# Loading replicated rows with one transfer per piece over all partitions instead of one per block of partitions

## The reference

```
e  = stack(tbl_f[ids[:, f]] for f in 0..38)              # (512, 39, 16)
z0 = relu(einsum('bhd,bkd,hks->bsd', e, e,  w0) + b0)     # 128 maps; first 64 are x1, the rest is summed
z1 = relu(einsum('bhd,bkd,hks->bsd', e, x1, w1) + b1)     # x2 and a summed half
z2 = relu(einsum('bhd,bkd,hks->bsd', e, x2, w2) + b2)     # all 128 summed
z  = sum over d of (z0[64:], z1[64:], z2)                 # 256 numbers per sample
y  = relu(relu([z, dense_ctx] @ W1 + c1) @ W2 + c2) @ W3
```

## Time and profile before

| | |
|---|---|
| median of the runs | 657.21 us |
| the profiled execution | 660.38 us, its span 658.6 us |
| granted TensorE clock over the span | 0.987 of full speed |
| TensorE matmuls busy | 613.0 us, 93% of the span |
| VectorE, ScalarE, GpSimd busy | 83%, 62%, 81% |
| moved by DMA | 78.60 MB, a mean of 119 GB/s |
| SyncE's DMA queue | 75.11 MB, 54.9% of the time of 16 DMA engines |

### The profile page before, as it was taken

How to read it: one execution, slowest core, us unless ns; L and a number is a source line. 1 busy time by engine, 2 the same in 40 slices (tenths; PEclk the granted TensorE clock), 3 DMA queues, 4 the chain that set the end, 5 groups by cost and what they waited for, 6 DMA issues and landing times.

```text
span 658.6 us, 6385 instructions
## 1 busy us (share of the span) xinstructions
PE 613.0 (93%) x1996; PEld 378.3 (57%) x1996; DVE 546.7 (83%) x616; ACT 410.6 (62%) x553; POOL 536.2 (81%) x325
## 2 busy tenths in 40 slices
PE   0169899999999999999999999999999999999998
PEld 0026465666656566656666666666566666655563
DVE  1248699898989898998989898989989898969740
ACT  2025857676676758576766757586777667575622
POOL 6657899898989899998989998999989886747520
PEclk9998899999999999999999999999999999999899
DMA  6689794938374756749384747567494847420000
GB/s 220 136 191 187 160 172 98 180 73 184 89 147 109 139 104 132 148 101 179 71 165 107 146 100 140 114 126 154 95 180 75 162 110 134 96 46 1 0 0 0
DMA packets 53216, 78.60 MB, mean 119 GB/s; under 512 B 39081, under 2 KB 42025, under 8 KB 49891
## 3 DMA queue, kind: packets, MB, share of 16 engines
q1 hardware_dynamic: 47566, 75.11, 54.9%
q0 software_dynamic: 5120, 1.29, 2.0%
q10 hardware_dynamic: 496, 1.80, 1.1%
HBM read 76.23 MB, written 1.94 MB: 119 GB/s over the span
## 4 chain that ended last, share of the span: by engine, by line
PE 38%; POOL 38%; ACT 11%; issue 6%; DMA 4%; DVE 3%; SPq 1%; DVEq 0%; ACTq 0%
POOL low L361 29%; PE z L681 20%; PE z L698 9%; POOL gat L351 9%; ACT x L448 7%; PE z L713 6%; ACT high L428 2%; DMA spread<-x_rows 2%; DVE prod L591 2%; DMA gat<-table_dram,index 2%; ACT r L472 1%; DMA x_rows<-gat 1%; DVE base L626 1%; DVE low L634 1%; PE base L758 1%
## 5 line engine op out<-in xcount | busy, mean ns | idle before, releaser
L361 POOL TENSOR_TENSOR low<-prod,high 128x1024 fp32r<-128x1024 f32 (+2 forms) x160 | 380.7, 2399 | 58.8 <-ACT high L428 57.7
L591 DVE TENSOR_TENSOR prod<-spread,x 128x1024 f32<-128x1024 f32 (+1 forms) x256 | 307.6, 1212 | 38.7 <-ACT x L448 37.7
L681 PE MATMUL z<-prod,w_sb 128*128 128x512 f32 (+3 forms) x608 | 294.0, 604 | 36.9 <-DVE prod L572 32.4
L428 ACT ACTIVATE high<-prod 128x1024 fp32r<-128x1024 f32 (+2 forms) x160 | 167.7, 1058 | 116.9 <-DVE prod L591 98.4
L698 PE MATMUL z<-high,high_w_L 128*128 128x512 f32 (+1 forms) x448 | 205.9, 459 | 1.0 <-ACT high L438 1.0
L713 PE MATMUL z<-low,high_w_L 128*128 128x512 f32 (+1 forms) x448 | 182.6, 488 | 5.5 <-POOL low L361 3.5
L681 PEld LDWEIGHTS z<-prod,w_sb 128*128 128x128 f32 (+3 forms) x608 | 116.2, 192 | 124.0 <-issue 101.6
L351 POOL DMA_INDIRECT gat<-table_dram,index x160 | 154.7, 967 | 37.0 <-issue 35.3
L698 PE MATMUL z<-high,low_w_L 128*128 128x512 f32 (+1 forms) x448 | 179.0, 400 | 0.0
L448 ACT ACTIVATE x<-z,bias_sb 64x512 f32<-64x512 f32 (+1 forms) x186 | 120.2, 646 | 15.1 <-PE z L681 7.4
L713 PEld LDWEIGHTS z<-low,high_w_L 128*128 128x128 f32 (+1 forms) x448 | 82.8, 190 | 71.7 <-issue 45.8
(11 more groups left out here) (37 smaller groups left out, 62.4 us busy)
## 6 DMA issues: line engine op xcount, KB each, us to landing
spread<-x_rows SPq DMA_DIRECT2D x139, 192.0 KB, 13.5
spread<-x_rows SPq DMA_DIRECT2D x30, 546.0 KB
spread<-x_rows SPq DMA_DIRECT2D x47, 256.0 KB, 4.2
spread<-x_rows SPq DMA_DIRECT2D x15, 468.0 KB
x0base<-x_rows SPq DMA_DIRECT2D x47, 78.0 KB
gat<-table_dram,index POOLq DMA_INDIRECT x160, 5.6
x_rows<-gat SPq DMA_DIRECT2D x16, 72.0 KB, 2.2
wt_sb<-wt_dram SPq DMA_DIRECT2D x2, 512.0 KB, 19.0
```

Of the source, the lines that this page charges most:

```text
L361: pool.tensor_tensor(low[0:rows, h, 0:k, :], prod[0:rows, slot(c, kind, g), 0:k, :], high[0:rows, h, 0:k, :].bitcast(F32), ALU.subtract).t ...
L428: act.activation(high[0:rows, split_slot(c, kind, g), 0:k, :], prod[0:rows, slot(c, kind, g), 0:k, :], ACT.Copy).then_inc(high_ready, 1)
L591: dve.tensor_tensor(prod[0:rows, slot(c, kind, g), :, :], spread[0:rows, c % 2, g, :].unsqueeze(1).to_broadcast([rows, k, N]), x[0:rows, : ...
L681: last = pe.matmul(z[:, :], w[0:rows, at + j, :], prod[0:rows, slot(c, kind, g), j, :], start=g == 0 and j == 0, stop=closes and j == k - 1)
```

## The change

Every load of replicated rows becomes one transfer over all its partitions: one for `x0base` and one for `spread0` (117 partitions each), and one for each piece of `spread` (128 partitions), so 5 per chunk in place of 18. Their source patterns get a dimension in front: the three or four blocks. All of them are issued by SyncE, those of chunk 0 too; ScalarE's two helpers go. Semaphore counts follow (16 per transfer). The last blocks are loaded at full length (7 rows for 6, 10 for 9). `ROWS` is written another way and is 59 as before, so `store_x0` is unchanged.

```
-            def load_base(c, js=range(DPT)):
+            def load_base(c):
 ...
                 row = x0_dram[c, 0:1, 0:1]
-                for j in js:
-                    sp.dma_start(x0base[j * F:(j + 1) * F, :], bass.AP(row.tensor, row.offset, [[N, F], [1, N]])
-                                 ).then_inc(base_in, 16)
+                sp.dma_start(x0base[:, :], bass.AP(row.tensor, row.offset, [[0, DPT], [N, F], [1, N]])
+                             ).then_inc(base_in, 16)
 ...
-            def load_spread0(c, at, end, done, js=range(DPT)):
+            def load_spread0(c, at, end, done):
 ...
-                for j in js:
-                    many = min(end, DELTAS - j * T0) - at
-                    row = x0_dram[c, j * T0 + at:j * T0 + at + 1, 0:1]
-                    src = bass.AP(row.tensor, row.offset, [[N, F], [1, many * N]])
-                    sp.dma_start(spread0[j * F:(j + 1) * F, at:at + many, :].rearrange("p t n -> p (t n)"), src
-                                 ).then_inc(done, 16)
+                row = x0_dram[c, at:at + 1, 0:1]
+                src = bass.AP(row.tensor, row.offset, [[T0 * N, DPT], [N, F], [1, (end - at) * N]])
+                sp.dma_start(spread0[0:R0, at:end, :].rearrange("p t n -> p (t n)"), src).then_inc(done, 16)
 ...
-                for q in qs:
-                    many = min(end, F - q * G1) - at
-                    row = x0_dram[c, q * G1 + at:q * G1 + at + 1, 0:1]
-                    src = bass.AP(row.tensor, row.offset, [[0, QUAD], [1, many * N]])
-                    sp.dma_start(spread[q * QUAD:(q + 1) * QUAD, c % 2, at:at + many, :].rearrange("p g n -> p (g n)"),
-                                 src).then_inc(spread_in[p][c % 2], 16)
+                row = x0_dram[c, at:at + 1, 0:1]
+                src = bass.AP(row.tensor, row.offset, [[G1 * N, FPT], [0, QUAD], [1, (end - at) * N]])
+                sp.dma_start(spread[:, c % 2, at:end, :].rearrange("p g n -> p (g n)"), src
+                             ).then_inc(spread_in[p][c % 2], 16)
 ...
-            load_first()
             take_base(0)
-            load_first_spread()
```

More of the change, by code:

```diff
@@ L31 @@
 R0_LAST = (DPT - (DPT * T0 - DELTAS)) * F
-ROWS = F + FPT * (-(-(DELTAS - 1) // FPT))
+ROWS = F + FPT * (-(-max(DPT * T0 - 1, FPT * -(-F // FPT) - F) // FPT))
 G0 = -(-T0 // 2)
@@ L270, in load_base, with load_spread @@
                 row = x0_dram[c, 0:1, 0:1]
-                for j in js:
-                    sp.dma_start(x0base[j * F:(j + 1) * F, :], bass.AP(row.tensor, row.offset, [[N, F], [1, N]])
-                                 ).then_inc(base_in, 16)
-            def load_spread0(c, at, end, done, js=range(DPT)):
+                sp.dma_start(x0base[:, :], bass.AP(row.tensor, row.offset, [[0, DPT], [N, F], [1, N]])
+                             ).then_inc(base_in, 16)
+            def load_spread0(c, at, end, done):
                 if c >= 1:
                     sp.wait_ge(prod_done, PROD_NUMBER[c - 1, "L0", G0 - 1])
-                for j in js:
-                    many = min(end, DELTAS - j * T0) - at
-                    row = x0_dram[c, j * T0 + at:j * T0 + at + 1, 0:1]
-                    src = bass.AP(row.tensor, row.offset, [[N, F], [1, many * N]])
-                    sp.dma_start(spread0[j * F:(j + 1) * F, at:at + many, :].rearrange("p t n -> p (t n)"), src
-                                 ).then_inc(done, 16)
-            def load_spread(c, p, qs=range(FPT)):
+                row = x0_dram[c, at:at + 1, 0:1]
+                src = bass.AP(row.tensor, row.offset, [[T0 * N, DPT], [N, F], [1, (end - at) * N]])
+                sp.dma_start(spread0[0:R0, at:end, :].rearrange("p t n -> p (t n)"), src).then_inc(done, 16)
+            def load_spread(c, p):
                 at, end = PIECES[p]
@@ L312, in _ @@
             store_x0(0)
-            load_base(0, (0, 1))
+            load_base(0)
             for n, (at, end) in enumerate(FIRST_CUTS):
-                load_spread0(0, at, end, spread0_first[n], (0, 1))
+                load_spread0(0, at, end, spread0_first[n])
             for p in range(len(PIECES)):
-                load_spread(0, p, (0, 1))
+                load_spread(0, p)
             store_x0(1)
@@ L387, in split_weights @@
                                ).then_inc(high_w_ready, 1)
[L389 to L411, removed]
             def take_base(c):
-                act.wait_ge(base_in, 16 * DPT * (c + 1))
+                act.wait_ge(base_in, 16 * (c + 1))
                 if c >= 1:
@@ L565, in product0 @@
                     if c >= 1:
-                        dve.wait_ge(spread0_in, 16 * DPT * c)
+                        dve.wait_ge(spread0_in, 16 * c)
                 for n, (at, _) in enumerate(FIRST_CUTS):
                     if c == 0 and 2 * g == at:
-                        dve.wait_ge(spread0_first[n], 16 * DPT)
+                        dve.wait_ge(spread0_first[n], 16)
                 free_slot(c, "L0", g)
@@ L582, in wait_factors @@
                     if g == at and kind == "L1":
-                        dve.wait_ge(spread_in[p][c % 2], 16 * FPT * (c // 2 + 1))
+                        dve.wait_ge(spread_in[p][c % 2], 16 * (c // 2 + 1))
             def product(c, kind, g):
```

## The result

The changed kernel takes 1001.47 us (median of 4 runs, 999.87 to 1006.96), the kernel before 658.0 us in the same comparison. The ratio is 1.523, 95% interval 1.516 to 1.531: half as slow again. The forecast was 1310 us in a range of 980 to 1650. The direction and the small number of engines were right. The size was not: 1310 us is 31% too high, and the measured time lies near the lower edge of a wide range, close to rival B (990 us), which had a chance of 0.17.

A forecast was written before the change was run, and what follows sets the result against it. TensorE was taken to bound the kernel before, loads on three or four engines the changed one. Sixteen chunks at 73.0 us, fifteen gaps of 4, 24 at the start and 60 at the end gave 1312, stated as 1310 us, range 980 to 1650.

The forecast's parts named there:

- rival B: Loads of `spread`: confined to few engines, but these run free at 24.8 GB/s; 990 us in all, chance 0.17.
- The bound before: Steady state of the kernel before: TensorE busy 36.9 of 37 us sets the stage, DMA has 37% to spare.
- Three or four engines: All merged loads: the source's first count limits the cut, so 3 engines carry `x0base` and `spread0`, 4 carry `spread`.
- `x0base` and `spread0`, 25.7 us: Layer 0's loads per chunk on three engines at 24.8 GB/s each: 3.2 us for `x0base`, 22.5 us for `spread0`.
- `spread`, 46.5 us: Pieces of `spread` per chunk, 655 KB on the busiest engine at 14.1 GB/s; 26.4 us at 24.8 GB/s.
- The gap of 4 us: Between chunks: `x0base` waits for the store behind the last piece, so the three engines idle 4 us per stage.
- The ends: Start and tail of the span: first data at 24 us, and 60 us after the last piece has landed.
- Rival A: All merged loads: the cut follows the partitions alone, 16 or 13 engines, start 5 to 6 us sooner; 652 us, chance 0.13.

## Why the prediction was right, and where its size was off

**The bound before, right.** Runs that shorten the loads move nothing, runs that lengthen them past a stage move everything.

**Three or four engines, right, and now shown.** This was inferred from 39 rows on 13 engines. Three marks per `x0base`, 0.52 of the engines with a count of 8, and stages that grow with counts of 4 and 2 show it, at a fixed destination in the cases of 8 and 4. The Trainium skill (DMA: Bandwidth & Descriptors, "Why a DMA increments its semaphore by 16 and not by 1") has exactly this rule, and every run agrees. Its advice in "Rules for kernel authors" to use one transfer over 128 partitions and not two over disjoint halves does not carry over to this case by itself: merging was harmless with 39 in front and cost 147 us with 3.

**`x0base` and `spread0`, 25.7 us, right.** From the issue at 370.24 to the product at 397.83 pass 27.6 us, 28.3 in the mean of 15 stages, start and landing among them.

**`spread`, 46.5 us: the term that was mis-sized.** From layer 0's first product, when `spread0` is there, to the first use of the last piece pass 27.8 us in the mean of 15 stages (32.3 once, otherwise 25.2 to 29.8), near the 26.4 of rival B. I took the 14.1 GB/s of the 32-partition pieces for four engines because two of them walk partitions 0 to 63 side by side. The rate belonged to 13 to 16 engines that share one block of 32 partitions; eight on the same partitions have 25.1. My argument against B, that a sixth of the engines rested and the others were no faster, was wrong: 13 engines still shared one limit, about 190 GB/s together. The Trainium skill (SBUF — State Buffer, "Door 1: The DMA port swizzle") puts 32 partitions on 8 ports with 218 GB/s in all; 209 with eight engines and 190 with more agree. It also has partitions 0 to 31 and 32 to 63 on the same ports, and the long slow stretches (15.8, 17 and 17 GB/s, some 4 to 8 us) appear where engines work 32 apart; where four share a block, only some 2 us at the start are slow. I had assumed that such engines stay slow; they reach 25 GB/s within the same piece. That they are slow while they walk in step and slip out of it fits all this, but no run shows it, and the slow stretch in the middle of a piece shows that the pace can drop again.

**The gap of 4 us, right.** The next `x0base` is issued 1.4 us after the last piece is first used, in the mean, and its data move over 1 us later. The DMA share is 0.02 from 427 to 430 us. With 28.3 and 27.8 us these 1.4 us make 57.5 of the stage's 57.7. So some 3 us are empty, less than the 4.5 us that the run with the early store was expected to win.

**The ends, right.** The last piece is first used at 940.9 us of 1000.1: 59 us to the end for the 60 taken. The span is 20.7 us to the first issue, 15 x 57.7, and 113.9 from the last issue to the end, of which 54.7 are the last chunk's loads.

**Rival A** fell with the changed kernel's three marks and stages of 57.7 us. Its gain at the start did not come either: with 13 engines over the whole width the third product of chunk 0 begins at 35.7 us, not at 31. That load ran on 13 engines; 16 engines over 128 partitions for `spread` would need a source that begins with a larger count than its four blocks, and was not tried.

## What to carry to other kernels

Before merging transfers, write down the first count of both patterns: a replicating or blocked source with 3 or 4 in front left 12 or 13 engines idle here, and exchanging two dimensions (with the matching weight order) can bring them back. Then compare bytes per stage with engines x 25 GB/s. A low DMA share next to idle compute engines can mean few busy DMA engines and no spare ones.

A rate measured with many engines on a narrow target can belong to the target. Ask how many engines share it before carrying it to a transfer with fewer.

## What the runs showed of the hardware that was not expected

- Eight engines move no less into 32 partitions than the usual split over all, 209 GB/s against 190, and leave the other half idle (DMA share from 184 to 221 us 0.48, where it was 0.63).
- Two engines writing 32 partitions apart have stretches at about 17 GB/s each between stretches at 25, without any change in the kind of load in flight.
- A store's issue on SyncE can last 30.5 us where loads on a few engines stand ahead of it; the same instruction took 0.6 us (median) in the kernel before.
